# One tanh over four heads in place of two, in the softcap attention of a seven-stage network

## The reference

```python
x = x + _L0_attn_a_ref(_layernorm(x, axis=-1), L0_attn_a_Wq, L0_attn_a_Wk, L0_attn_a_Wv, L0_attn_a_Wo)
...
att = jnp.einsum('bhqd,bhkd->bhqk', q, k) * scale
att = SOFTCAP * jnp.tanh(att / SOFTCAP)
att = jnp.where(causal[None, None], att, -jnp.inf)
att = jax.nn.softmax(att, axis=-1)
y = jnp.einsum('bhqk,bhkd->bhqd', att, v)
return y.transpose(0, 2, 1, 3).reshape(b, t, NH * HD) @ Wo
```

## Time and profile before

| | |
|---|---|
| median of 3 runs | 2919.26 us (2914.34 to 2929.24) |
| the profiled execution: its time | 2915.69 us |
| its span, first to last instruction | 2914.0 us |
| softcap attention's inner loop, within the span | about 115 to 432 us |
| mean granted TensorE clock, whole span | 0.918 |

### The profile page before, as it was taken

One profiled execution on the slowest core, in us unless ns is written; L12 is line 12 of the kernel. 1 busy time (PEld: TensorE's weight loads), 2 busy tenths in 40 slices (PEclk: granted clock), 3 DMA queues, 4 the chain that ended last, 5 costly groups with the idle time before them and its releaser, 6 DMA issues. The chain is left out here.

```text
span 2914.0 us, 68812 instructions
## 1 busy us (share of the span) xinstructions
PE 2469.1 (85%) x25231; PEld 1667.2 (57%) x25320; DVE 1960.1 (67%) x4292; ACT 1710.9 (59%) x3452; POOL 856.4 (29%) x1233
## 2 busy tenths in 40 slices
PE   8887878788888788888888888878999687899998
PEld 4433336643333276445555555557888466888898
DVE  5488886667787466698888888874333355566652
ACT  2588874324454453388788788853332334677778
POOL 2244332121111121255555555520000222232223
PEclk9999888878999889999999999989999777899999
DMA  4533302244243022522140222004000658622210
GB/s 173 156 80 79 72 7 72 87 115 59 38 50 45 1 78 96 142 25 31 16 46 2 31 31 30 2 7 174 1 1 2 105 140 158 101 30 33 43 35 8
DMA packets 280879, 175.04 MB, mean 60 GB/s; under 512 B 204768, under 2 KB 241136, under 8 KB 278512
## 3 DMA queue, kind: packets, MB, share of 16 engines
q1 hardware_dynamic: 271392, 162.45, 26.7%
q10 hardware_dynamic: 9168, 8.41, 1.2%
HBM read 111.75 MB, written 54.66 MB: 57 GB/s over the span
## 5 line engine op out<-in xcount | busy, mean ns | idle before, releaser
L1481 ACT ACTIVATE ad_e<-ps,ad_nm 128x1024 f32<-128x1024 f32 (+7 forms) x512 | 380.2, 744 | 113.0 <-DVE ad_nm L1566 107.8
L1566 DVE TENSOR_REDUCE ad_nm<-ps 128x1 f32<-128x1024 f32 (+7 forms) x512 | 372.1, 752 | 43.8 <-PE ps L1414 31.5
L719 ACT ACTIVATE ab_e<-ps 128x512 f32<-128x512 f32 (+3 forms) x384 | 167.0, 490 | 194.9 <-PE ps L634 194.0
L1412 PE MATMUL ps<-fd_k_st,fd_q_st 96*128 96x512 bf16 (+3 forms) x768 | 215.9, 341 | 56.8 <-ACT ad_e L1481 51.2
L1595 DVE CUSTOM_DVE_ANT_0 ad_t<-ad_e,ad_rz 128x128 f32<-128x128 f32 (+7 forms) x256 | 208.2, 813 | 41.3 <-POOL ad_e L1531 24.1
L1531 POOL TENSOR_SCALAR ad_e<-ad_e,ad_c 128x128 f32<-128x128 f32 (+7 forms) x256 | 191.9, 749 | 19.3 <-DVE ad_c L1583 17.8
L1427 PE MATMUL ps<-ident,ad_t 128*128 128x128 f32 x1152 | 170.9, 276 | 26.3 <-ACT ad_prT L1491 12.7
L2007 POOL TENSOR_TENSOR st_it_low<-st_it,st_it_high 128x256 fp32r<-128x256 f32 x128 | 98.5, 783 | 315.2 <-ACT st_it_high L2270 309.7
L1491 ACT ACTIVATE ad_prT<-ps 128x128 f32<-128x128 f32 (+7 forms) x256 | 166.3, 650 | 21.4 <-PE ps L1435 21.3
L1522 POOL TENSOR_SCALAR_AFFINE_SELECT ad_e<-ad_e 128x128 f32<-128x128 f32 x256 | 90.7, 354 | 299.6 <-ACT ad_e L1481 274.4
L724 ACT ACTIVATE aa_e<-ps 128x1024 f32<-128x1024 f32 (+1 forms) x192 | 150.3, 824 | 38.0 <-PE ps L634 35.3
(11 more groups left out here) (383 smaller groups left out, 7096.0 us busy)
## 6 DMA issues: line engine op xcount, KB each, us to landing
scr_a<-pa_parts SPq DMA_DIRECT2D x24, 512.0 KB, 2.7
fa_q_st<-scr_a SPq DMA_DIRECT2D x24, 512.0 KB, 7.8
split<-f_split SPq DMA_DIRECT2D x16, 768.0 KB, 3.9
fd_q_st<-scr_d SPq DMA_DIRECT2D x48, 256.0 KB, 8.0
g_w<-split SPq DMA_DIRECT2D x8, 1536.0 KB, 17.8
scr_d<-pd_parts SPq DMA_DIRECT2D x20, 384.0 KB, 2.8
st_w_first<-split ACTq DMA_DIRECT2D x5, 1536.0 KB, 8.1
fa_k_st<-scr_a SPq DMA_DIRECT2D x24, 256.0 KB, 8.5
```

The lines of the kernel that those rows point to most:

```text
L719: act.activation(e[:, u % ER, h, lo:QB], m.ps[:, n4(u, h) % 3, lo:QB], ACT.Exp, scale=scale).then_inc(s_read[0], 1)
L1412: last = pe.matmul(m.ps[:, bank, 0:n], q_st[:, b, 2 * h + s, t * P:(t + 1) * P], k_st[:, b, s, cc * QB:cc * QB + n], start=True, stop=True)
L1481: act.activation(e[:, u % EB, s, 0:L], src, ACT.Exp, bias=nm[:, u % EB, s:s + 1], accum_out=z[:, u % EB, s:s + 1]).then_inc(exped[s], 1)
L1566: dve.tensor_reduce(nm[:, u % EB, s:s + 1], src, AX.X, ALU.max, negate=True).then_inc(maxed[s], 1)
```

## The change

One tanh per step reads all four heads from banks 0 to 3, and waits for one semaphore that the last of four score matmuls raises. The four score matmuls of a step are issued together, at the place of `scores(0)`, and wait until the whole tanh of the step before has been read; at the place of `scores(1)` nothing is issued. The exponential's wait is on the remaining semaphore. What each matmul and each activation computes is the same, and the plain attention, which shares the code, keeps its order.

```diff
@@ scores(p), TensorE
+                    if not plain and p == 1:
+                        return
                     if not plain:
-                        wait(pe, s_read[p], i, PER, u)
-                    for h in (2 * p, 2 * p + 1):
+                        wait(pe, s_read[0], i, PER, u)
+                    for h in (2 * p, 2 * p + 1) if plain else range(HG):
                         bank = n4(u, h) % 3 if plain else h
@@ from_scores and exponential, ScalarE
-                for p in range(2):
-                    wait(act, s_ready[p], i, PER, u + 1)
-                    act.activation(e[:, u % ER, 2 * p:2 * p + 2, lo:QB], m.ps[:, 2 * p:2 * p + 2, lo:QB], ACT.Tanh,
-                                   scale=scale / softcap).then_inc(s_read[p], 1)
+                wait(act, s_ready[0], i, PER, u + 1)
+                act.activation(e[:, u % ER, :, lo:QB], m.ps[:, 0:HG, lo:QB], ACT.Tanh,
+                               scale=scale / softcap).then_inc(s_read[0], 1)
 
             def exponential(i, u):
                 g, par, s, qb, kt, lo = place(u)
-                wait(act, s_read[1], i, PER, u + 1)
+                wait(act, s_read[0], i, PER, u + 1)
```

## The result

The changed kernel is slower: 2934.56 us median (2922.32 to 2949.83, 13 runs) against 2921.71 (2914.34 to 2937.69, 13 runs), ratio 1.0052 with a 95% interval of 1.0032 to 1.0071. By the ratio that is some 15 us, with an interval of 9 to 21, just over the 0.5% I had called the bound; the two medians are 12.9 us apart. I had forecast no change (2920, range 2907 to 2934, 0.84 for no change, 0.10 for slower). The forecast was wrong in both: the median lies outside the range, and the loss is beyond its interval.

The account below looks back on a forecast made before the run. ACT and DVE were taken as both full in full steps. Saved starts were spent as waits, about 0 per group; with 1.5 us for the lower clock, rounded to 1, and 3.6 to the median: 2920 us, range 2907 to 2934.

Parts of the forecast that it names:

- The saved starts: On ACT, one tanh of 2048 for a pair: 0.05 us saved per step, 4.8 us over 96 steps.
- The floor of the round trip: Tanh to scores to tanh after short exponentials, at s0, s1, s4, s5: 2.3 us exposed per group, 18 over eight.
- the 230.0 - 228.5 of the prediction: At the next group's s0: scores behind weigh of s8 allow the tanh at 230.0; ACT would be free at 228.5.
- s3 to s6: Within a group: about 0.5 us won from s3 to s4, 0.5 lost from s4 to s6.
- The boundary: Between two groups, s11 to the next s0: still held by an accrue, stays as it is, nothing won.
- The sum: Whole kernel: 0 at 2.4 GHz plus 1.5 at the lower clock, rounded to 1 us.
- the cover of the round trip in full steps: Full steps: round trip of 1.37 us hidden under the exponential's 1.80, with 0.43 to spare.
- the sentence on the clock: PE's same work in bigger pieces: effect on the clock taken as nothing, since PE's work per step stays the same.
- a sign of being wrong: Tanhs of 2048 waiting for PE in full steps would show that the cover is gone.
- The rival on the slower side: Exposed round trip on top, at s0, s1, s4, s5: +13, or +22 with the lower clock, 2941; chance 0.10.

Follow-up runs that it names:

- first experiment: The changed kernel with only the merged tanh undone: two tanhs, scores still waiting for the whole step; 2936.49 us, ratio 1.0059.
- the mask cut: Mask product over 1 of 128 columns per head, most masking left out: kernel before 2893.30 us (0.9902), changed kernel 2911.52 us (0.9965).
- the extra matmuls: Eight unread matmuls per group, four each behind weigh at s4 and s5: changed kernel 2928.39 us (1.0023), kernel before 2928.22 us (1.0020).
- The pair of runs that differ only in their waits: Two tanhs, both score pairs ahead of weigh: whole-step waits 2936.49 us (1.0059), release pair by pair 2921.29 us (0.9991).

## Why the prediction was wrong

*The saved starts* were right in size. In the changed trace a tanh of 2048 that waits for nothing takes 338.85 - 337.09 = 1.76 us to the next start, as computed. Undoing the merge (first experiment) made the loop 5.5 us longer and the time by 2 us, within its interval, so their worth of 4.8 us fits the traces and is too small for the runs. The changed kernel loses in spite of them.

*The floor of the round trip* was right at each of its places. From the changed trace, s4 to s5 takes 3.18 us where I had 3.13; s5 to s6 3.71 for 3.56; s0 to s1 3.04 for about 2.95. With the mask cut, the idle time ahead of the tanh is 0.34 us at s4 in six of the eight groups (I had 0.42), 0.79 at s5 (0.84), 0.63 at s1 (0.6), and 1.49 at s0 in five groups, which is the 230.0 - 228.5 of the prediction. The same trace has 0.97 to 1.07 at s7 in all groups but the first, where I had nothing.

*s3 to s6.* I expected 0.5 won (s3 to s4) and 0.5 lost (s4 to s6). Between s3 and s6 the averages are 9.73 before and 9.82 after. The sum is right, and by luck: nothing was won (2.94 and 2.93), and only 0.10 lost (6.79 and 6.89).

*The boundary* I had at nothing won or lost. It lost 0.70 us a group. I had worked it out in a group in which the accrue already held it, and took that one for all; in three of seven it didn't. After the change it does in nearly all. The short mask removes the accrue's part, and 1.0 us between s11 and s0 is still there, now the round trip behind weigh of s8 and the half projection. So the failure is one of the sample: one boundary stood for eight.

*The sum* took 1.5 as 1, which is of no account here.

*The step that failed most* is the cover of the round trip in full steps, "1.37 us against its 1.80 in full steps: hidden, 0.43 to spare", together with the sentence on the clock: "what that does to the clock I can't bound by a row, and take it as nothing". At s7 it was 2.95 us from the exponential's start to the tanh (338.85 to 341.80), not 1.37. The prediction had named this as a sign of being wrong: tanhs of 2048 that wait for PE in full steps. s6 to s7 is a full step by its width only. Its slots also carry projection and denominators, which I had named in the kernel's description and in no term of the sum. Counted from the rows above: scores 1.20, weigh 0.61, projection 1.13, denominators 1.06, scores 1.19 are 5.19 us at 2.4 GHz. ACT leaves 5.20: from 335.45, where the scores of s6 can start, to 337.09 + 1.76 + 1.80 = 340.65, where the tanh of s7 could. So even there nothing was to spare but what overlaps; with the extra matmuls, where the clock stayed up, the step did take 3.56 us with the mask cut. At 1.2 GHz the projection alone is 2.08. And with the change the lower clock comes right there: in s4 and s5 PE now works in one piece and then idles until a whole tanh is read, 4.12 us busy in 6.70 in the stretch shown, and the clock fell in s6 in all groups but the first, where the kernel before kept it. Over the loop the time at 1.2 GHz rose from 72 to 93 us. That the lumpier work is what lowers the clock is argued from these rows; that the low clock lengthens the step is shown by the extra matmuls. The place costs 1.22 x 8 = 10 us of the loop's 16. The extra matmuls took 0.98 off s6 to s7, and 13 us off the loop (8.3 with the mask cut).

*The rival on the slower side* ("the exposed round trip comes on top") had the cause right, the change's wait for a whole step, on PE, and its places only in part. I gave it 0.10 for thinking that accruals would hide it. The pair of runs that differ only in their waits speaks for it. With the cut masks its places, s0, s1, s4 and s5, carry 1.87 of the 2.66 us by which a group is longer; in the two kernels as they are they carry 0.97 of 2.07, and s7, which it doesn't name, carries more. That the measured 15 lies between its +13 and +22 is therefore partly luck.

What stays open: how the loss splits exactly between clock and round trip in the whole kernel's time, since the time behind the loop differs from trace to trace by more than that; what decides in which groups the clock falls; and why the extra matmuls cost the kernel before some 6 us.

## What to carry to other kernels

Merging two instructions that read separate buffers also merges their releases; with a single set of banks, the producer can't start before the whole read has ended, nor the reader before the whole production. Price that as a round trip at every slot, with all else that the producer's queue holds in that slot, and not in a typical step. Sample a wait in each of its repetitions before calling it fixed: a boundary that is held in four groups of seven isn't held. And where a change makes the matmuls come in larger lumps, give the clock a term or a rival of its own, read from rows of the steps around the change; here it was taken as nothing, and a wait of 1 to 1.9 us a group came of it together with the queue.

## What the runs showed of the hardware

- One activation of 128x2048 out of four PSUM banks ran at the rate of two of 128x1024: 1.76 us to the next start against 1.81 for the pair.
- Eight matmuls a group that nothing reads made the changed kernel some 8 us faster (1.0023 against 1.0052), with the granted clock at 1.00 over a stretch where it was 0.52 without them; they made the kernel before some 6 us slower (1.0020). Ahead of the falls shown PE had been busy for 4.12 of 6.70 us; with the extra matmuls, for 5.89 of 6.70, and it didn't fall. Other groups kept the clock after 4.18 and 4.97 of 6.70.
- The same instructions behind the loop took 2463 us at a granted clock of 0.921 and 2486 at 0.910.
- An affine select on GpSimd took 1269 ns on average here and 634 in the plain attention, for the same 128x512 elements; what makes the difference no run separates.
